# Layer three of a graph kernel: the bias as a bf16 product, the last gathered pair inside the last dense turn, and four address lists brought early

## The reference

```python
for _ in range(3):                                   # three mean layers
    x = segment_sum(x[src], dst) / max(counts, 1)
x = layernorm(x0 + x)
mlp = lambda x: layernorm(relu(relu(relu(x@W0+b0)@W1+b1)@W2+b2) @ Wo + bo) * w + b
fs, fr = flux_mlp(x[src]), flux_mlp(x[dst])          # 64 -> 128
a = a_mlp((x[src] + x[dst]) / 2)                     # 64 -> 64
flux = 0.5 * (einsum(fs, nvec) + einsum(fr, nvec)) - 0.5 * a * (x[src] - x[dst])
x = layernorm(x + (x + segment_sum(flux, dst)))
```

## Time and profile before

| what | value |
|---|---|
| time, median of 3 runs | 9919.28 us |
| span of the profiled execution, first to last instruction | 7229.7 us |
| what lies around the span, by difference to the median | 2689.6 us |
| layer three, first to last dense product | 796.4 us |
| from there to the first gather of the edge pass | 31.5 us |
| gathers of the edge pass | 4051.3 us |
| mean granted TensorE clock | 0.884 |

### The profile page before, as it was taken

How to read it: one execution, slowest core, us unless ns; L and a number is a source line. 1 busy time by engine, 2 the same in 40 slices (tenths; PEclk the granted TensorE clock), 3 DMA queues, 4 the chain that set the end, 5 groups by cost and what they waited for, 6 DMA issues and landing times. The chain is left out here.

```text
span 7229.7 us, 163080 instructions
## 1 busy us (share of the span) xinstructions
PE 5477.3 (76%) x50180; PEld 4418.6 (61%) x50180; DVE 4804.5 (66%) x9663; ACT 2615.2 (36%) x5447; POOL 5207.0 (72%) x5066
## 2 busy tenths in 40 slices
PE   2699999999999999956666666666666666666665
PEld 1699999999999999934444444444444444444443
DVE  6899898922222545466777777777777777777776
ACT  0688888810000111123333333333333333333332
POOL 4588888757776666567777777777777777777774
PEclk6799999999999999968888888888888888888887
DMA  5334333356666666656666666666666666666664
GB/s 157 118 138 141 133 136 137 136 200 228 218 223 212 225 219 225 206 142 159 169 165 165 166 169 165 166 165 168 165 166 165 169 165 165 165 169 165 165 165 107
DMA packets 598091, 1226.27 MB, mean 170 GB/s; under 512 B 328767, under 2 KB 406347, under 8 KB 580569
## 3 DMA queue, kind: packets, MB, share of 16 engines
q0 software_dynamic: 212704, 619.72, 32.9%
q1 hardware_dynamic: 369306, 570.23, 23.1%
q10 hardware_dynamic: 15471, 29.03, 1.3%
HBM read 1020.76 MB, written 197.70 MB: 169 GB/s over the span
## 5 line engine op out<-in xcount | busy, mean ns | idle before, releaser
L1826 POOL DMA_INDIRECT edge_rows<-node_table,edge_et x3224 | 3067.9, 952 | 984.6 <-issue 937.5
L1843 PE MATMUL edge_tp<-ident,edge_yc 128*128 128x128 f32 x1612 | 530.0, 349 | 1423.6 <-ACT edge_h L1926 1385.9
L855 POOL DMA_INDIRECT two_rows<-x_parts,src_at x1120 | 1077.0, 962 | 533.9 <-issue 357.6
L1342 PE MATMUL two_acc<-x_parts,win 128*128 128x192 bf16 x16072 | 1384.9, 247 | 19.0 <-issue 12.8
L1342 PEld LDWEIGHTS two_acc<-x_parts,win 128*128 128x128 fp8e4 x16072 | 1341.6, 98 | 30.8 <-issue 20.8
L1918 ACT ACTIVATE edge_yc<-edge_rows 128x512 f32<-128x512 f32 x403 | 253.7, 630 | 2676.6 <-DMA edge_rows<-node_table,edge_et 2640.8
L1843 PEld LDWEIGHTS edge_tp<-ident,edge_yc 128*128 128x128 f32 x1612 | 279.4, 173 | 1514.4 <-issue 1316.7
L1854 PE MATMUL edge_mp<-edge_h,edge_W 128*128 128x512 f32 x1612 | 1184.5, 877 | 2.0 <-ACT edge_h L1926 2.0
L1087 ACT ACTIVATE win<-one_count 128x784 fp8e4<-128x784 f32 x1312 | 1069.1, 825 | 145.0 <-PE one_count L1038 82.5
L855 POOL DMA_INDIRECT one_rows<-x_parts,src_at x560 | 868.2, 1550 | 176.9 <-issue 170.1
L2048 DVE TENSOR_REDUCE edge_ssq<-edge_sq 128x8 f32<-128x512 f32 x403 | 276.4, 686 | 996.3 <-ACT edge_sq L1933 996.3
(11 more groups left out here) (328 smaller groups left out, 7530.0 us busy)
## 6 DMA issues: line engine op xcount, KB each, us to landing
win<-adjacency SPq DMA_DIRECT2D x80, 3136.0 KB
adjacency<-win SPq DMA_DIRECT2D x41, 3136.0 KB
edge_near<-near_ids SPq DMA_DIRECT2D x403, 192.0 KB
edge_rows<-node_table,edge_et POOLq DMA_INDIRECT x3224
two_rows<-x_parts,src_at POOLq DMA_INDIRECT x1120
node_table<-two_row SPq DMA_DIRECT2D x49, 322.0 KB
edge_own<-node_table SPq DMA_DIRECT2D x46, 322.0 KB
node_sums<-edge_seg SPq DMA_DIRECT2D x806, 16.2 KB
```

The costliest lines, as they stand in the source:

```text
L855: pool.indirect_dma_start(rows[:, b % 2, e, :], None, XP.rearrange("p (j c) -> (p j) c", c=3 * C), bass.IndirectOffsetOnAxis(ap=src_at[:, ...
L1342: mm = pe.matmul(acc[b][:, half * 3 * C:(half + 1) * 3 * C], win[:, b, half, j, :].bitcast(FP8), now[:, j, :], start=(j == 0), stop=(j == ...
L1826: pool.indirect_dma_start(rows[:, h.b, t, :], None, T5, bass.IndirectOffsetOnAxis(ap=et[:, h.b, 0, t:t + 1].bitcast(I32), axis=0))\
L1843: pe.matmul(to, yc[:, h.b % 2, 2 * pr:2 * pr + 2, :].rearrange("p t c -> p (t c)"), ident[:, :], is_transpose=True, start=True, stop=False)
```

## The change

The bias of the output product becomes three bf16 parts that stand in rows 0, 32 and 64 of a 128-row operand with zeros elsewhere, and the ones become a 128x128 bf16 operand; the product stands ahead of the wait for the last relu. The gathered pair that finishes with the last dense turn is worked through PE inside that turn, at products 92 to 164, and the dense pair before it at 12 to 84 (before: 120 to 192); the last gathered block is summed at the end of the turn before. For this the last ten turns of PE stand outside its loop. For the last two items `flux` is cut in two (`flux_in`, `flux_out`), and the y parts and products with x (`flux_in`) stand ahead of the variance. SP stores y parts and x ahead of the table row, which alone waits for `row_done`. The first four index lists of the edge pass (`EARLY`) are loaded in layer three, into a tile and with eight semaphores that are held around both stages; the clearing of these and its barrier come after the edge pass.

```diff
+            with semaphores(nc) as ahead_sem, nc.sbuf_tensor("edge_et", [P, RB, 4, TL], F32) as et:
+                et_in = [ahead_sem(f"edge_et_in{b}") for b in range(RB)]
...
-        bo2, ones = sb("bo2", [1, 2, 2 * C]), sb("ones", [1, P])
+        bo_parts, bo_rest = sb("bo_parts", [P, 3, 2 * C], BF16), sb("bo_rest", [P, 2 * C])
+        bo3, ones = sb("bo3", [P, 2, 2 * C], BF16), sb("ones", [P, P], BF16)
...
-            def node(it):
+            def node(it, final=False):
+                if final:
+                    flux_root(it.n - 1)
                 act.wait_ge(sems["squares"], it.n + 1)
...
             def store(it):
                 sp.wait_ge(sems["y3_done"], it.n + 1)
-                sp.wait_ge(sems["row_done"], it.n + 1)
                 sp.sem_inc(storing, 1)
...
+                sp.wait_ge(sems["row_done"], it.n + 1)
+                sp.sem_inc(storing, 1)
...
             chunks(sp, step, DP, 2 * PARTS)
+            for c in range(EARLY):
+                sp.dma_start(et[:, c, :, :].rearrange("p f t -> p (f t)"),
+                             ET[:, c % 4, c // 4 * 4 * TL:(c // 4 + 1) * 4 * TL]).then_inc(et_in[c], 16)
...
             def last(it):
-                pe.wait_ge(sems["h_ready"], 3 * it.n + 3)
                 if from_item(it, 2):
                     pe.wait_ge(sems["o_used"], it.n - 1)
                 to = flux_ps[it.b2].rearrange("p j c -> p (j c)")
-                pe.matmul(to, ones[0:1, :], bo2[0:1, :, :].rearrange("p j c -> p (j c)"), start=True, stop=False)
+                pe.matmul(to, ones[:, :], bo3[:, :, :].rearrange("p j c -> p (j c)"), start=True, stop=False)
+                pe.sem_inc(issued, 1)
+                pe.wait_ge(sems["h_ready"], 3 * it.n + 3)
                 pe.matmul(to, hT[2][:, :], WO[:, :, :].rearrange("p h c -> p (h c)"), start=False, stop=True).then_inc(sems["o_ready"], 1)
...
+                begins = (120, 20)
+                if ending and h.c == DP - 1:
+                    due, begins = items(h.back(1)) + items(h)[:1], (92, 12)
...
+                if ending and h.c == DP - 2:
+                    edge_sums(pe, h, sel, rows, edge_acc, sel_ready, fetched, edge_made, used, layer)
...
-            chunks(pe, lambda h: step(h, 1), DP, 2 * PARTS)
-            for it in items(Chunk(0, DP - 1, 2 * PARTS)):
-                for run in stages:
-                    run(it)
+            chunks(pe, lambda h: step(h, 1), DP - 2 * PARTS, 2 * PARTS)
+            for c in range(DP - 2 * PARTS, DP):
+                step(Chunk(0, c, 2 * PARTS), 1, True)
+            for run in stages:
+                run(items(Chunk(0, DP - 1, 2 * PARTS))[1])
...
-            nodes(Chunk(0, DP - 1, 2 * PARTS))
-            variance(PAIRS - 1)
-            flux(PAIRS - 1, (PAIRS - 1) % RN, (PAIRS - 1) // RN, (PAIRS - 1) % 2, True)
+
+            last_edges, last_pair = items(Chunk(0, DP - 1, 2 * PARTS))
+            dve.wait_ge(used, 2 * BLKS)
+            norm(last_edges, edge_pairs, edge_made)
+            m, slot, turn, b2 = before(last_edges)
+            flux_in(m, slot, turn, True)
+            flux_out(m, slot, b2)
+            m, slot, turn, b2 = before(last_pair)
+            flux_in(m, slot, turn, True)
+            variance(m)
+            flux_out(m, slot, b2)
+            dve.wait_ge(summed, 2 * DP)
+            norm(last_pair, pairs_of(acc[1 - (DP - 1) % 2]), made, True)
+            m = last_pair.n
+            flux_in(m, m % RN, m // RN, True)
+            variance(m)
+            flux_out(m, m % RN, m % 2)
...
-            for c in range(AHEAD):
-                sp.dma_start(et[:, c, :, :].rearrange("p f t -> p (f t)"),
-                             ET[:, c % 4, c // 4 * 4 * TL:(c // 4 + 1) * 4 * TL]).then_inc(et_in[c], 16)
```

More of the change, by code:

```diff
@@ L1243, in node @@
                 if from_item(it, 1):
-                    flux_root(it.n - 1)
+                    if not final:
+                        flux_root(it.n - 1)
                     act.wait_ge(sems["y_ready"], it.n)
@@ L1256, in nodes @@
                     node(it)
-            chunks(act, nodes, DP, 2 * PARTS)
+            chunks(act, nodes, DP - 1, 2 * PARTS)
+            for it in items(Chunk(0, DP - 1, 2 * PARTS)):
+                node(it, it.n == PAIRS - 1)
             flux_root(PAIRS - 1)
@@ L1317, in last, with step @@
                 to = flux_ps[it.b2].rearrange("p j c -> p (j c)")
-                pe.matmul(to, ones[0:1, :], bo2[0:1, :, :].rearrange("p j c -> p (j c)"), start=True, stop=False)
+                pe.matmul(to, ones[:, :], bo3[:, :, :].rearrange("p j c -> p (j c)"), start=True, stop=False)
+                pe.sem_inc(issued, 1)
+                pe.wait_ge(sems["h_ready"], 3 * it.n + 3)
                 pe.matmul(to, hT[2][:, :], WO[:, :, :].rearrange("p h c -> p (h c)"), start=False, stop=True).then_inc(sems["o_ready"], 1)
             stages = (turn, first, lambda it: hidden(it, 1), lambda it: hidden(it, 2), last)
-            def step(h, layer):
+            def step(h, layer, ending=False):
                 b, now = (h.b2 + layer) % 2, parts[1 - layer]
@@ L1333, in step @@
                 due = items(h.back(1)) if layer and not early(h, 1) else []
+                begins = (120, 20)
+                if ending and h.c == DP - 1:
+                    due, begins = items(h.back(1)) + items(h)[:1], (92, 12)
                 for at in range(2 * J):
                     half, j = at // J, at % J
-                    if at == J and not early(h, 1):
+                    if at == J and not early(h, 1) and not (ending and h.c == DP - 1):
                         edge_sums(pe, h.back(1), sel, rows, edge_acc, sel_ready, fetched, edge_made, used, layer)
-                    for it, begin in zip(due[::-1], (120, 20)):
+                    for it, begin in zip(due[::-1], begins):
                         if at >= begin and (at - begin) % 18 == 0 and (at - begin) // 18 < len(stages):
@@ L1399, in _ @@
                 oi.link(dve.tensor_copy(WO[r, half, :], wo[r, :]))
-            oi.link(dve.tensor_copy(bo2[0:1, :, :], bo[0:1, :].unsqueeze(1).broadcast_to([1, 2, 2 * C])))
+            split3(oi, dve, bo[:, :], [bo_parts[:, i, :] for i in range(3)], bo_rest[:, :])
+            oi.link(dve.memset(bo3[:, :, :], 0.0))
+            for i in range(3):
+                r = slice(NW * i, NW * i + 1)
+                oi.link(dve.tensor_copy(bo3[r, :, :], bo_parts[r, i, :].unsqueeze(1).broadcast_to([1, 2, 2 * C])))
             oi.link(dve.tensor_scalar(WY[:, :], WY[:, :], 0.5, None, ALU.mult))
@@ L1409, in _, with flux_in @@
             LINKS, FIRST_LINKS = 26, 10
-            def flux(m, slot, turn, b2, full):
+            def flux_in(m, slot, turn, full):
                 y = row[:, slot, :, X_Y:X_Y + C]
@@ L1427, in flux, with flux_out @@
                 dve.sem_inc(sems["y3_done"], 1)
+            def flux_out(m, slot, b2):
                 dve.wait_ge(sems["std_ready"], m + 1)
@@ L1445, in variance, with norm @@
                 dve.sem_inc(sems["var2"], 1)
-            def norm(it, sums, done):
-                oi.at(base + it.n * LINKS - (LINKS - FIRST_LINKS) if from_item(it, 1) else base)
+            def norm(it, sums, done, final=False):
+                if not final:
+                    oi.at(base + it.n * LINKS - (LINKS - FIRST_LINKS) if from_item(it, 1) else base)
                 own = xn[:, it.slot, :, :]
@@ L1459, in root @@
                     dve.sem_inc(sems["squares"], 1)
-                    if from_item(it, 1):
+                    if from_item(it, 1) and not final:
                         variance(it.n - 1)
@@ L1482, in nodes @@
                         m, slot, turn, b2 = before(it)
-                        flux(m, slot, turn, b2, from_item(it, RN + 1))
+                        flux_in(m, slot, turn, from_item(it, RN + 1))
+                        flux_out(m, slot, b2)
             chunks(dve, nodes, DP - 1, 2 * PARTS)
-            nodes(Chunk(0, DP - 1, 2 * PARTS))
-            variance(PAIRS - 1)
-            flux(PAIRS - 1, (PAIRS - 1) % RN, (PAIRS - 1) // RN, (PAIRS - 1) % 2, True)
+            last_edges, last_pair = items(Chunk(0, DP - 1, 2 * PARTS))
[7 more added lines that the diff above has]
+            variance(m)
+            flux_out(m, slot, b2)
+            dve.wait_ge(summed, 2 * DP)
[4 more added lines that the diff above has]
+            flux_out(m, m % RN, m % 2)
 def bring(nc, X, x3):
@@ L1727, in edge_pass @@
         ring = lambda name, n: [sem(f"{name}{b}") for b in range(n)]
-        et_in, gathered = ring("et_in", RB), ring("gathered", RB)
+        gathered = ring("gathered", RB)
         near_in, yd_in = ring("near_in", 4), ring("yd_in", 4)
@@ L1784, in step @@
                     sp.sem_inc(sems["storing"], 1)
-                if not early(h, AHEAD):
+                if not early(h, EARLY):
                     sp.dma_start(et[:, h.b, :, :].rearrange("p f t -> p (f t)"),
```

29 lines of the change are left out of this document (14 added, 15 removed).

## The result

The kernel after takes 9846.74 us, the median of 4 runs (9809.87 to 9864.07); the kernel before, on the same chip, 9922.78 us (4 runs, 9918.13 to 9949.02). The ratio is 0.9914, 95% interval 0.9887 to 0.9941: 76 us faster, where 38.5 were forecast, and outside the range of 9869 to 9900.

The account below looks back on a forecast made before the run. PE's order was taken to bound layer three and POOL's gathers the edge pass. -31.5 - 1.6 - 6.9 + 0.7 + 0.8 = -38.5 us, so 9919.3 became 9881 us (9874 to 9889; wider range 9869 to 9900).

Parts of the forecast that it names:

- The span is 2689.6 us short of the median, and I take what lies around it as unchanged: Whole kernel: the profiled span's saving of 38.5 us was carried straight to the median of 9919.3 us.
- PE is busy in 792.2 of them: Layer three: of its 796.4 us PE is busy in 792.2, so PE's order and no wait sets its length.
- The bias product, -31.5: Layer three's dense turns: the bf16 bias over 128 rows saves 0.67 us an item, 47 items, -31.5 us (-15 to -33).
- the clock's cost of waits in the last turn: Layer three's last turn: PE's waits of 2.85 and 1.2 us can lower the clock, +0.8 us (0 to 1.7).
- Rival 1: Bias product: only the passes are saved and the idles stay, 47 x 0.32 = 15.0 us; 9897 us, chance 0.10.
- The extra increment and wait for the last relu cost nothing: Output product in layer three: the relu still has 18 products, 1.49 us, before it, so cost is zero.
- Rival 2: Layer three: the gathers show through, POOL's hiccups of 20 us all land on PE; 9901 us, chance 0.07.
- Rival 3: Edge pass: gathers get slower as tiles move in on-chip memory; at 25 ns a gather 9961 us, chance 0.04.
- Rival 4: Layer three's ten straight turns each stall as at a round's end, 16.2 us comes back; 9897 us, chance 0.05.
- the loop's end: Ten turns outside PE's loop in layer three: one of two round's ends goes, -1.6 us (0 to -2.7).
- The last turn and the border, -6.9 + 0.7 + 0.8 = -5.4: Layer three's end to first edge gather: earlier tail work and lists -6.9, one more clearing +0.7, clock lost in waits +0.8 us.

Follow-up runs that it names:

- nog_bias: The kernel before with only the bf16 bias product, its wait moved behind it, and without layer three's 560 gathers: 9236.56 us.
- nog_rows: The kernel before without layer three's gathers, its f32 bias product over 128 rows of which 127 are zero: 9269.46 us.
- again: The kernel before, unchanged, run for a second profile and the spread of its times: ratio 0.9993.
- split: The kernel after with each block of 14 gathers in layers two and three cut in two: 9717.57 us against 10153.31 for the kernel before, ratio 0.9563.
- again_b: The kernel before, unchanged, once more for its profile, on another chip than the first runs: 10213.35 us.

## Why the prediction was wrong

**The step that failed** is the sentence "The span is 2689.6 us short of the median, and I take what lies around it as unchanged", and with it that the sum is made from that one execution. The sign came out right, and the size was half of what was measured. Nothing lies around the span; the executions that are timed spend those us inside, in stages where PE's order alone is not what sets a turn's length. The prediction's "PE is busy in 792.2 of them" does not hold there: PE is busy 1024.7 of 1470.1, and a turn is a block of gathers, then what PE has left of the turn. So the term that was mis-sized is the bias product's -31.5: alone it took 96.5 us off layer three (74.4 in the second set).

**The bias product, -31.5.** Its size is right where nothing is held up: 32.7 in the stage, with a slot of 0.54 in nog_bias (0.11 from the bias to the output product, 0.22 between its passes, 0.22 to the next dense product) where I had 0.57. In the timed executions its work still counts nearly whole (28 to 32 us), since `last` lies in the stretch that POOL waits for. What the sum lacks is the clock in that stretch, 42 to 61 us; the sum has only the clock's cost of waits in the last turn.

**Rival 1** (only the passes are saved) is out: nog_rows saves no pass and takes 14.7 us off, 0.31 an item. The Trainium skill, TensorE: Matmul & The Clock Gate, "Step-by-step: what each phase is for", says of a weight load that its timing follows the columns and that the row count doesn't matter. The loads agree, two of one row in 0.29 us and two of 128 rows in 0.30; what 128 rows take off are the idles beside the loads, so that the rows earn nothing, as the prediction drew from it, does not follow. The Trainium skill, TensorEngine Tiling (Array Packing), Key Properties, has a change of tiling mode drain TensorE. The idle of 0.16, which stays with one row in either type, fits that, if one row counts as another mode, which no run here shows; the 0.33 behind the product, which shrinks with the type alone, asks for more than that rule.

**"The extra increment and wait for the last relu cost nothing".** In the quiet stage it holds. In the kernel after PE stands 60.8 us ahead of the output product, for 29.9 of them waiting for the relu, but in the kernel before it stands 38.5 ahead of the bias for the same late relu. The order was not tried apart from the product.

**Rival 2** (the gathers show through) had the right engine at the wrong price: the prediction let hiccups of 20 us a layer through, and the gathers hold up the instructions of the others for most of 17.2 us a block.

**Rival 3** (slower gathers in the edge pass) is out: 949 ns a gather after, 952 in the second profile of before, as against the earlier trace rows.

```profile
L1863 POOL DMA_INDIRECT edge_rows<-node_table,edge_et x3224 | 3060.9, 949 | 2312.4 <-DMA edge_et<-edges_turned 1111.8 <-issue 925.2 <-DMA x_parts<-x_parts 251.0
```

**Rival 4, and the loop's end** (-1.6): no gap was seen in the last turn outside its waits, but the effect of one round's end is lost in the stops of the held-up turns and was not tested apart.

**The last turn and the border, -6.9 + 0.7 + 0.8 = -5.4.** This part has no gathers beside it, and it came nearly as worked out. From DVE's first reduce of the last turn to the first gather it took 51.0 us before (both profiles) and 45.25 after (4309.61 to 4354.86): -5.8. PE's two waits are 2.69 and 0.96 (2.85 and 1.2 forecast). The last pair's reduce comes 27.4 us after that first reduce, 26.1 before; the dense end is 6.6 us later in the turn, 5.1 forecast. The clock fell to 1.2 GHz around the first wait:

```profile
4312.00:4319.70 7.70, 5.29 (x42) 5.09 (x43) 5.85 (x22) 1.23 (x4) 0.00 (x0) 0.78 0.09 21
```

That is 3.4 us at 1.2 GHz, some 1.7 of work, where the sum took half of it. After, answering to the earlier trace rows (start, duration, names, idle before):

```profile
4337.01 0.56 DVE L1480 TENSOR_REDUCE two_xw<-two_acc 128x128 f32<-128x384 f32 x1 [0.22 <-DVE two_row L1465]
4344.84 0.42 PE L1330 MATMUL two_flux<-two_bo,two_ones 128*128 128x256 bf16 x1
4345.50 1.22 PE L1333 MATMUL two_flux<-two_WO,two_h 128*128 128x256 f32 x2 [0.24 <-ACT two_h L1257]
...
4348.02 0.17 DVE L1455 RECIPROCAL two_ssq<-two_ssq 128x2 f32<-128x2 f32 x1 [0.42 <-ACT two_ssq L1242]
4350.40 0.37 SPq L1287 DMA_DIRECT2D node_table<-two_row  x1
4354.86 0.96 POOL L1863 DMA_INDIRECT edge_rows<-node_table,edge_et  x1 [0.50 <-issue]
```

The bias stands ahead of the relu's wait, DVE waits 0.42 for the last root and takes the reciprocal at once, and one transfer is left for SP. POOL gathers 0.84 us after its block's first instruction (4354.02), where the prediction had half a microsecond; before, it waited 2.56 for lists.

**What stays open.** Why POOL's gathers hold up PE and ACT in every later profile and did not in the first; no run changed that, and none tells POOL's own work from the transfers that it starts. Also open is how two one-row f32 passes go with a longer time at 1.2 GHz: the runs show that either half of the change takes some 83 us of it away, not by what.

## What to carry to other kernels

Compare a profile's span with the time of its own execution and with the median before using any row of it: a gap of a quarter is an open question, and "it lies inside" has to stand among the rivals. Where blocks of gathers hold up the other engines, price an edit by whether it lies in the stretch that releases the next block, and count that stretch's clock; cutting the blocks was worth some 350 us on top of the edit, about four times the edit itself (an estimate: 436, less 0.0086 of 10153, since the kernel after was not run on that chip).

## What the runs showed of the hardware

In the timed executions that were profiled, some 6 us into a block of POOL's gathers PE's instructions come in steps of 0.7 us, and they come freely again 1.6 to 2.6 us after its last gather (again and split). A relu of ACT started 11.8 us after its product was done. With pieces of seven gathers PE's idle time in layer two with no cause that the profile names falls from 358.4 us (again) to 197.5 (split). The gathers themselves take the same time as ever (950 ns on average in layers two and three of again, 962 in the first profile). The same kernel takes 9898 and 9906 us in sets of runs on two chips, and 10153 and 10213 in two sets on a third; of the 311 us between the spans of again and again_b, 176 lie in the edge pass, 91 ahead of layer two and 26 in it.
